# Feed-forward with the gated product and its rounding in PSUM, each chunk closed in its own step

## What is computed

```python
x = x + tanh(g_xattn[0]) * wkv(layernorm(x), ctx)          # a recurrence along the sequence
x = x + tanh(g_ffn[0])   * ffn(layernorm(x))               # 512 -> 2048 -> 512, activations in int8 groups of 64
x = x + tanh(g_xattn[1]) * attention(layernorm(x), ctx)    # 16 heads; queries and output quantised per row
x = x + tanh(g_ffn[1])   * linear(rmsnorm(x))              # ternary weights

def ffn(x):                                                # w1, w2, w3 are signs times one scale
    h = silu(q(x) @ w1.T) * (q(x) @ w2.T)                  # q: per group of 64, x / s, rounded, times s
    return q(h) @ w3.T

def attention(x, ctx):                                     # output: qdq(o) @ qdq(wp).T + bp
    ...
```

## Time and profile before

| | |
|---|---|
| median of 3 runs | 1131.3 us (1129.19 to 1131.79) |
| the profiled execution, its own time | 1129.28 us |
| its span | 1127.5 us |
| PE busy | 854.5 us (76%) |
| DVE busy | 881.2 us (78%) |
| ACT busy | 572.4 us (51%) |
| POOL busy | 566.2 us (50%) |
| granted TensorE clock, mean | 0.893 of full |

### The profile page before, as it was taken

How to read it: one execution, slowest core, us unless ns; L and a number is a source line. 1 busy time by engine, 2 the same in 40 slices (tenths; PEclk the granted TensorE clock), 3 DMA queues, 4 the chain that set the end, 5 groups by cost and what they waited for, 6 DMA issues and landing times.

```text
span 1127.5 us, 15927 instructions
## 1 busy us (share of the span) xinstructions
PE 854.5 (76%) x4503; PEld 375.1 (33%) x4503; DVE 881.2 (78%) x1453; ACT 572.4 (51%) x1024; POOL 566.2 (50%) x559
## 2 busy tenths in 40 slices
PE   1376867672997888888888895589898898965654
PEld 1233534431443444444443343122232222222221
DVE  3859999994988988889888874577777777735985
ACT  1366969562443554445444455255555555644442
POOL 1166877861334444444444434264564655645652
PEclk9668889886998999999999998599999999986786
DMA  8422524330332322222222223212122121000011
GB/s 303 154 84 76 170 101 159 104 102 19 60 62 47 57 47 47 47 51 52 47 47 47 55 55 91 81 38 73 48 71 67 47 73 41 1 1 1 37 56 56
DMA packets 132708, 78.12 MB, mean 69 GB/s; under 512 B 90656, under 2 KB 115376, under 8 KB 132656
## 3 DMA queue, kind: packets, MB, share of 16 engines
q1 hardware_dynamic: 132656, 77.51, 25.6%
HBM read 37.50 MB, written 12.58 MB: 44 GB/s over the span
## 4 chain that ended last, share of the span: by engine, by line
DVE 41%; PE 26%; issue 16%; ACT 8%; SPq 4%; POOL 2%; DMA 1%; DVEq 1%; ACTq 0%; POOLq 0%
PE bank L1132 4%; DVE B L1532 4%; PE bank L1105 4%; DVE B L1422 4%; DVE B L1424 3%; DVE B L1427 3%; PE bank L1122 3%; PE bank L1037 3%; DVE B L1425 3%; SPq L403 3%; PE bank L1046 2%; DVE B L1339 2%; DVE B L1416 2%; DVE B L1433 2%; ACT B L791 2%
## 5 line engine op out<-in xcount | busy, mean ns | idle before, releaser
L1037 PE MATMUL bank<-A,B 128*128 128x512 f16 x1024 | 233.7, 382 | 15.4 <-DMA B<-B 15.4
L1532 DVE TENSOR_REDUCE B<-bank 128x1 f32<-128x512 f32 x256 | 163.4, 684 | 72.9 <-PE bank L1105 71.6
L878 ACT ACTIVATE A<-bank 128x512 f32<-128x512 f32 x256 | 138.9, 593 | 89.3 <-PE bank L1122 86.6
L531 POOL TENSOR_TENSOR B<-B 128x512 f16<-128x512 f32 x64 | 73.9, 1155 | 192.3 <-ACT B L768 89.4
L1037 PEld LDWEIGHTS bank<-A,B 128*128 128x128 f16 x1024 | 101.0, 99 | 140.0 <-issue 21.3
L613 POOL TENSOR_TENSOR B<-A 128x512 f32<-128x512 f32 x64 | 79.4, 1271 | 132.7 <-ACT A L878 132.7
L1046 PE MATMUL bank<-A,B 128*128 128x512 f16 x512 | 132.8, 407 | 1.3 <-DMA B<-B 1.3
L763 ACT ACTIVATE B<-B 128x512 f32<-128x512 f32 x64 | 40.4, 631 | 179.3 <-DVE B L1427 179.3
L1105 PE MATMUL bank<-A 96*128 96x512 f16 x256 | 101.0, 405 | 15.4 <-DVE B L1532 10.3
L1122 PE MATMUL bank<-A 98*128 98x512 f16 x256 | 96.6, 391 | 13.1 <-DMA A<-B 8.1
L1422 DVE SCALAR_TENSOR_TENSOR B<-bank,ffs,B 128x512 f32<-128x512 f32 x64 | 48.0, 751 | 50.4 <-PE bank L1037 24.1
(11 more groups left out here) (228 smaller groups left out, 1718.4 us busy)
## 6 DMA issues: line engine op xcount, KB each, us to landing
B<-in_L_ffn_w_dram SPq DMA_DIRECT2D x48, 256.0 KB, 3.3
A<-k_parts SPq DMA_DIRECT2D x48, 128.0 KB, 2.5
A<-B SPq DMA_DIRECT2D x192, 32.0 KB, 1.9
X<-in_x_dram SPq DMA_DIRECT2D x4, 1024.0 KB, 14.2
B<-in_ctx_dram SPq DMA_DIRECT2D x4, 1024.0 KB, 7.9
k_parts<-B SPq DMA_DIRECT2D x16, 256.0 KB, 2.2
v_rows<-B SPq DMA_DIRECT2D x16, 256.0 KB, 2.0
B<-v_rows SPq DMA_DIRECT2D x16, 256.0 KB, 3.2
```

Of the source, the lines that this page charges most:

```text
L531: nc.gpsimd.tensor_tensor(HLb[j][:, 1, :], Db[j % 2], HLb[j][:, 0, :], ALU.subtract).then_inc(lo_done, 1)
L878: nc.scalar.activation(PR[(HG * t + j) % 8], bank[2 + j % 2][:, :], ACT.Exp, scale=SCALE).then_inc(exp_done, 1)
L1037: last = mm(bank[2 * n + q][:, :], XQT[a][:, m, :], wt[:, m % DB, j * 512:j * 512 + 512], start=(m == 0), stop=(m == 2 * DB - 1))
L1532: reduce(NMX[:, t, j:j + 1], bank[n % 2][:, :], AX.X, ALU.max, negate=True).then_inc(row_max, 1)
```

## The change

1. The gated product is written in place into `bank[2 + q]`; `Hb` goes. The group maximum and the scaling read it there. ACT's rounding reads `Tb` (SBUF) and writes `bank[q]`; `scaled` reads it there. So `bank[q]` is free for PE's chunk `c + 2` at `d_done` (it was `silu_done`), and `bank[2 + q]` at `t_done` (it was `h_done`).
2. DVE's step `c` is now `hidden(c)`, one middle operation in three of four chunks, `scaled(c)`, and then the side jobs. ACT's step is side jobs, `round_up(c)`, `silu(c + 1)`, `high(c)`.
3. `prep_max` loses its product, which becomes `prep_quant`. The query's steps are laid out anew over chunks and tiles: the projection, `q_full`, `q_bias` and `q_low` come one tile later than before.
4. The output bias is added by POOL in attention, one tile at the end of each group, and no more in the feed-forward.

The numbers of instructions of each kind don't change otherwise.

```diff
@@ POOL, in tiles(k, last)
                     for j in range(FC):
                         if j == 0 and there(i - 3):
-                            x_bias(i - 3)
-                        if j == 0 and there(i - 2):
-                            q_rstd(i - 2)
+                            q_diag(i - 3)
                         if j == 1 and not (last and a == 1):
                             x_turned(pool, k, a)
                             prep_lo(i + 1)
                         if j == 1 and not last:
                             prep(i + 2)
-                        if j == 3 and there(i - 2):
-                            q_diag(i - 2)
+                        if j == 2 and there(i - 2):
+                            q_rstd(i - 2)
+                        if j == 2 and there(i - 4):
+                            q_low(i - 4)
                         lo_part(i, j)
-                        if j == 3 and there(i - 3):
-                            q_low(i - 3)
@@ POOL, in add_weights, at the end of each group
+                    rows = X[:, bass.ds(n, 1), :].rearrange("p a d -> p (a d)")
+                    nc.gpsimd.tensor_tensor(rows, rows, bp_all[:, :], ALU.add).then_inc(x_biased, 1)
@@ ACT
             def round_up(c, q):
                 act.wait_ge(t_done, c + 1)
-                nc.scalar.activation(Tb[q], Tb[q], ACT.Copy, bias=RND).then_inc(u_done, 1)
+                act.wait_ge(silu_done, c + 1)
+                nc.scalar.activation(bank[q][:, :], Tb[q], ACT.Copy, bias=RND).then_inc(u_done, 1)
@@ ACT, in tiles: the new list of a step
+                        if j == 0 and there(i - 3):
+                            q_round(i - 3)
                         if more and j == 0:
                             prep_round(i + 1)
                         if more and j == 1:
                             x_turned(act, k, a)
                             prep_hi(i + 1)
+                        if j == 1 and there(i - 4):
+                            q_bias(i - 4)
                         if j == 2 and not last:
                             prep_norm(i + 2)
+                        if j == 3 and there(i - 2):
+                            q_norm(i - 2)
                         if j == 3 and there(i - 3):
+                            q_operands(i - 3)
+                        round_up(c, j % 2)
+                        if more or j < FC - 1:
+                            silu(c + 1, (j + 1) % 2)
+                        high(i, j)
@@ PE, in up and in tiles
-                        up_to(pe, silu_done, c - 1)
+                        up_to(pe, d_done, c - 1)
                     else:
-                        up_to(pe, h_done, c - 1)
+                        up_to(pe, t_done, c - 1)
...
                         up(i, j, k, a, FC * i + j)
-                        if j == 1 and there(i - 3):
+                        if j == 0 and there(i - 4):
+                            q_project(i - 4)
+                        if j == 2 and there(i - 3):
                             q_turn(i - 3)
-                        if j == 2 and there(i - 3):
-                            q_project(i - 3)
@@ DVE
+                H = bank[2 + q][:, :]
                 dve.wait_ge(b_ps, c + 1)
                 dve.wait_ge(silu_done, c + 1)
-                stt(Hb[q], bank[2 + q][:, :], C2, SAb[q], ALU.mult, ALU.mult).then_inc(h_done, 1)
+                up_to(dve, d_done, c)
+                stt(H, H, C2, SAb[q], ALU.mult, ALU.mult).then_inc(h_done, 1)
...
-                stt(grouped(Db[q]), grouped(Tb[q]), RND, spread(1), ALU.subtract, ALU.mult).then_inc(d_done, 1)
+                stt(grouped(Db[q]), grouped(bank[q][:, :]), RND, spread(1), ALU.subtract, ALU.mult).then_inc(d_done, 1)
@@ DVE, in tiles
-                        if j == 0 and not first:
-                            residual(i - 2, a)
-                        if not (first and n < 1):
-                            scaled(c - 1, (j + 1) % 2)
-                            dve.wait_ge(d_done, c)
                         hidden(c, j % 2)
                         if j == 0 and not (last and a == 1):
                             prep_scaled(i + 1)
-                        if j == 0 and there(i - 2):
-                            q_stats(i - 2)
-                        if j == 1 and not last:
-                            prep_stats(i + 2)
-                        if j == 2 and there(i - 3):
-                            q_full(i - 3)
-                        if j == 2 and there(i - 2):
-                            q_max(i - 2)
+                        if j == 1 and not first:
+                            residual(i - 2, a)
+                        if j == 3 and not last:
+                            prep_quant(i + 2)
+                        scaled(c, j % 2)
+                        if j == 0 and not last:
+                            prep_stats(i + 2)
+                        if j == 0 and there(i - 3):
+                            q_ints(i - 3)
+                        if j == 0 and there(i - 4):
+                            q_full(i - 4)
+                        if j == 1 and there(i - 2):
+                            q_stats(i - 2)
-                        if j == 3 and not last:
+                        if j == 2 and not last:
                             prep_max(i + 2)
                         if j == 3 and there(i - 2):
-                            q_ints(i - 2)
+                            q_max(i - 2)
```

More of the change, by code:

```diff
@@ L165, in flamingo_kernel @@
         SAb = [part(512, F32) for _ in range(2)]
-        Hb = [part(512, F32) for _ in range(2)]
         Tb = [part(512, F32) for _ in range(2)]
@@ L543, in q_diag @@
                 nc.gpsimd.tensor_tensor(DIAG, id32[:, :], QSC[:, 0:1].to_broadcast([P, P]), ALU.mult).then_inc(diag3, 1)
-            def x_bias(u):
-                pool.wait_ge(qs3, u + 1)
-                rows = X[:, bass.ds(u, 1), :].rearrange("p a d -> p (a d)")
-                nc.gpsimd.tensor_tensor(rows, rows, bp_all[:, :], ALU.add).then_inc(x_biased, 1)
             def q_low(u):
@@ L800, in _, with tiles @@
             prep_norm(1)
-            def tiles(k, first, last):
+            silu(0, 0)
+            def tiles(k, last):
                 for a in range(2):
@@ L1410, in prep_max, with prep_quant @@
                 ts(gsm[:, 7, :], gsm[:, 5, :], XUP, None, ALU.mult)
+            def prep_quant(i):
                 tt(grouped(PT), grouped(PXN), spread(6), ALU.mult).then_inc(xt_done, 1)
@@ L1469, in _ @@
             prep_max(0)
+            prep_quant(0)
             prep_stats(1)
@@ L1472, in _ @@
             prep_max(1)
+            prep_quant(1)
             def tiles(k, first, last):
@@ L1478, in tiles @@
                         c = FC * i + j
-                        n = FC * a + j
-                        if j == 0 and not first:
-                            residual(i - 2, a)
-                        if not (first and n < 1):
-                            scaled(c - 1, (j + 1) % 2)
-                            dve.wait_ge(d_done, c)
                         hidden(c, j % 2)
@@ L1507, in _ @@
             tiles(TOK // 2 - 1, False, True)
-            C = FC * TOK
-            scaled(C - 1, 1)
             residual(TOK - 2, 0)
-            dve.wait_ge(down_read, TOK - 1)
             q_stats(TOK - 2)
+            q_ints(TOK - 3)
+            q_full(TOK - 4)
+            q_max(TOK - 2)
+            residual(TOK - 1, 1)
+            q_stats(TOK - 1)
             q_full(TOK - 3)
-            q_max(TOK - 2)
             q_ints(TOK - 2)
-            residual(TOK - 1, 1)
-            dve.wait_ge(down_read, TOK)
-            q_stats(TOK - 1)
             link(ts(LSC, LSC, 1.0 / 127.0, None, ALU.mult))
             ts(LSC, LSC, TG[:, 3:4], None, ALU.mult).then_inc(area_free, 1)
+            q_max(TOK - 1)
             q_full(TOK - 2)
-            q_max(TOK - 1)
             q_ints(TOK - 1)
```

60 lines of the change are left out of this document (26 added, 34 removed).

## The result

The changed kernel takes 1074.08 us (median of 5, 1073.56 to 1081.12), the one before 1131.06 (1129.19 to 1131.79): a ratio of 0.9511, 95% interval 0.9492 to 0.953, 57 us less. The profiled execution took 1081.12 us, the longest of the five. (The quotient of the two medians alone is 0.9496.)

What follows compares the result with a forecast made beforehand. Neither PE nor DVE was full: they waited for each other, both losing. With 23.0 us a tile instead of 26.5, 12 tiles save 42.0, tile 15 0.5: 1129.3 - 42.5 = 1086.8, stated as 1088; range 1075 to 1108.

Steps and rivals of the forecast that it cites:

- PE's floor of 22.16 a tile: PE's matmul groups, projection and query turn in one tile: 22.16 us at full clock, taken as a floor.
- DVE's step: DVE in one chunk, `hidden` through rounding to `scaled`: 4.08 us, four 16.3; with 4.80 of other items, 21.1 a tile undisturbed.
- Contention left, 1.4 us: DVE beside POOL: L1410 meeting `lo_part` 1.0 us, L1425 0.1 in each chunk; DVE then 22.5 us per tile.
- From 22.5 to 23.0: Tiles 3 to 14: 23.0 us taken over floors of 22.2 (PE) and 22.5 (DVE), for little buffer and ACT's thin place.
- Tiles 0 to 2: nothing: First three tiles: no gain, because PE is full there.
- PSUM operands at no cost: DVE's and ACT's operations with a bank operand: no time added, from a reduce of 684 ns (bank) against 686 (SBUF).
- The rival with 70 ns each: Bank operands dearer: 16 operations a tile by 0.07 us, 24.1 us a tile, about 1100; chance 0.10.
- PE's 2.94 us ahead of the projection: PE's idle time before each query projection, laid to ACT's late copy in its queue: 2.94 us a tile would go.
- The disturbance only moves: Rival: two to three more DVE meetings with POOL or ACT's thin place, 25 us a tile, about 1111; chance 0.18.
- Tile 15 and the chain behind it: Last tile: first `hidden` to last `lo_part` 21.9 us, 0.5 less; then SP's loads, so the whole gain arrives at the end.
- The bias in attention for nothing: POOL's 16 additions of 1.27 to 1.72 us in attention cost nothing, covered by 14 waits, 107.4 us in all.
- The rival that the gate at `d_done` would make gaps: Slower: PE, gated in every chunk, idles and is granted 1.2 GHz part of the time; 1144 at f = 0.25; chance 0.04.

## Why the prediction was right, and where it was off

The direction, the place and the mechanism were right, the size was short by a quarter: 42.5 us forecast, 57 measured. The part that the granted clock had in the old tiles was not seen.

*PE's floor of 22.16 a tile.* Right to 0.1: 22.05 as the mean of the pairs in the loop (21.9 and 22.2), 22.1 in the kernel with L1407 moved, where PE alone sets the pace, and only a cut on both engines went below.

*DVE's step.* Right: 4.08 us forecast; in tile 11 the four steps, from `hidden` to the operation behind `scaled`, take 4.09, 3.99, 3.99 and 3.97. What follows them takes 5.0 without L1407's stretch and the loop's turn, where 4.8 was forecast. Together they make 21.0; the sum of 21.1 stood.

*Contention left, 1.4 us.* Over-sized, the first term that failed. L1407 was the one operation that met `lo_part`, as the prediction put it, but it lost 0.73, not 1.0 (0.90 against the 0.17 of its like), and L1426 lost 0.02 a chunk in the loop's tiles (249 ns against 231), not 0.1. In its place there are 0.2 a tile for the loop's turn, which had not been counted. Together that is 22.05, not 22.5.

*From 22.5 to 23.0.* This margin for two engines near their limit was wrong. The two banks and two buffers were enough: the changed kernel loses nothing between PE and DVE, with both full. It alone is 6 us. The whole way from 23.0 to the 21.93 that the 12 tiles take on average is 12.9 of the 15 us missing.

*Tiles 0 to 2: nothing.* They gained 2.1 us (63.1 to 61.1). PE's busy time had looked like the limit; the kernel with less work on PE, which has the same 19.9, 19.9, 21.2, shows that now DVE is.

*PSUM operands at no cost.* Right: 4 to 7 ns each, and 29 ns less on ACT. The rival with 70 ns each falls. The estimate from the Trainium skill (Perfetto Trace Analysis, Optimizing Scalar/DVE Operations) falls with it: no row here shows 65 ns more for a bank operand.

*PE's 2.94 us ahead of the projection.* They are gone, as forecast. But the prediction put them to the order of ACT's queue alone. With the operands in PSUM and the old queue most of them go as well (8.3 us in 12 tiles instead of 39.3), so the queue's order alone did not make them. And the pauses cost more than their length: the nine falls of the clock behind them were worth some 12 us. The prediction had them in its rows as a mean of 0.95 and read its tile's rows from one of the three tiles without a fall.

*The disturbance only moves.* One meeting a tile is left, which costs 0.7 us. The rival had two to three more.

*Tile 15 and the chain behind it.* Forecast 21.9 from its first `hidden` to `lo_part`; measured 21.8 (604.30 to 626.1). From there to the first exponential it takes 45.7 us, before 45.2: what the feed-forward gains arrives at attention.

*The bias in attention for nothing.* Right: 275.4 and 275.5 us of exponentials with and without. In the kernel with only the bias moved, POOL's 14 waits there shrink from 107.4 to 90.3 us, by 1.2 each. But "attention as long as before" did not hold for the changed kernel: it is 1.5 and 9.1 us longer in its two profiles, with the granted clock. That it held 20 us in the old order was not forecast as such; the 1.07 us of its stretch were, as a part of the sum.

*The clock.* The forecast that it would be full held: 1.00 in the 12 tiles. The rival that the gate at `d_done` would make gaps falls.

*The range.* Its low end was worked out from the profiled execution's 1129.28 us, without the 2 us that lift the forecast to the median. By the same terms it is 1078.7, so the measured median lies 4.6 us below what the prediction's own floor allows.

What the prediction didn't see is how much its parts overlap. It listed the collisions, the queue on ACT and the bias as terms, and their sum was about right for the whole, but any one part of the change would have brought 20 to 46 of these us of FF.

## What to carry to other kernels

When a group's mean is well above its minimum, look at what the engine that shares its memory does beside it: here three collisions in a row cost 2.4 us of a 26.9 us tile, and either another place in the order or an operand in PSUM removes most of it. When several edits aim at the same loss, make them one at a time: the second brings little. And when two engines look full, one extra operation on each, or one less, tells in a run which has slack; here neither had, so the next gain needs an edit on both.

## What the runs showed of the hardware that was not expected

- How little data a DVE operation has does not protect it: eight numbers per row (L1407) take 0.90 us instead of 0.17 when POOL's subtraction has begun before it.
- Which operation it is does. In the kernel before, the reciprocal of eight numbers (L1426) started 13 times about 0.1 us behind a long operation of POOL and took 0.20 each time, and the group maximum (L1424), whose operand is in SBUF too, took 0.685 to 0.687 in all 48 chunks, 14 of them begun behind POOL's. So an operand in SBUF alone does not make a stretch; of the large operations only those with two operands there were stretched.
- With one operand in a bank the product was not stretched beside POOL: 0.690 to 0.692 us, where with both in SBUF it took 1.36 to 1.51.
- A held operation ends at a fixed distance behind POOL's: the 24 products and 11 `prep_scaled` of the kernel before and the 11 `scaled` of the new order with SBUF operands all 0.55 us behind it (to 0.01), the 11 L1407 of the changed kernel 0.03.
- POOL's operation is longer in such a meeting too: `x_bias`, begun at 479.86 while the product was under way, takes 1.71 us; in attention it takes 1.26 to 1.28.
- The clock fell behind nine of 12 pauses of PE of 2.8 to 6.4 us in the kernel before, behind four of 12 of 1.8 to 5.6 us in the kernel with only the bias moved, and behind none of 0.8 us or less with the operands in PSUM. A fall lengthened its tile by some 1.3 us.
- Attention's first 60 us were granted 0.84 to 0.98 of the clock in profiles of the same work, and the first three groups differ by 8.8 us.
